# Turning a Mamba scan round: states on the partitions, channels and tokens along the free axis

## The chip, the cores and the metric

The kernel runs on one core of a Trainium2 chip. The metric is the device time of one execution in microseconds, from the first to the last instruction; lower is better. The core's engines are called PE (TensorE; its weight loads are listed as PEld), DVE (VectorE), ACT (ScalarE), POOL (GpSimd) and SP (SyncE, which issues the transfers here).

## What is computed

The kernel runs eight blocks one after the other on a residual of 2048 tokens by 128 features: a gated delta rule, a window attention, a Plücker attention, a ternary feed-forward, a flash attention, a mixture of experts, a bidirectional Mamba and an int8 feed-forward. Only the Mamba block is touched. Cut to what matters, it is, for both directions (m = 1 forward, m = 2 with the tokens flipped):

```
xp, z = split(x @ W_in.T);  xc = silu(causal_conv(xp) + conv_b)      # 256 channels
dt_lo, Bm, Cm = split(xc @ W_xp.T)                                   # 8, 64 states, 64 states
dt = softplus(dt_lo @ W_dt.T + dt_b);  A = -exp(A_log)               # A: 256 x 64
h  = exp(dt[:, :, None] * A) * h + (dt * xc)[:, :, None] * Bm[:, None, :]   # at each token
y  = einsum('ben,bn->be', h, Cm)                                     # sum over the 64 states
out = ((y + xc * Dp) * silu(z)) @ W_out.T
```

There are 8 sequences of 256 tokens. So h has 8 x 256 tokens x 256 channels x 64 states elements in each direction, and each of them goes once through a recurrence along the tokens.

## The kernel before

`bi_mamba` normalises the input, then calls `mamba_inputs`, `mamba_scan` and `mamba_output` for m = 1 and for m = 2. Each call is a block of its own: the next one starts when all engines have ended it. Within a block each engine has its own instruction list, and semaphores (`q[...]`) order the engines among one another.

`mamba_inputs` projects, convolves and makes dt and dtx = dt * xc, four column chunks of 512 tokens (`SCH`) one after the other, with channels on partitions (two halves of 128, `SE`). B and C are projected with their 64 states repeated, and split into three bf16 parts (`high`, `split`: lines 3148 to 3157, 3211 to 3217 and 3240 to 3250), so that TensorE can later copy one state's row to all partitions.

`mamba_scan` has channels on partitions. A step is one state n of one chunk c: 4 x 64 = 256 steps in each direction. In a step
- PE spreads the state's row of B over all partitions (`b_row`, two bf16 matmuls, L3351 and L3352), the row of C likewise (`c_row`), and adds the product hc into banks 0 and 1 (`add_up`, L3368, two f32 matmuls with the identity as weights; a matmul in f32 is listed as two weight loads and two MATMUL records);
- ACT takes the decay exp(A dt) from SBUF to PSUM (`decay`, L3412, two activations of 510 columns; the first token of each sequence keeps a decay of zero) and copies the rows of B (L3418) and part of that of C (L3423) to SBUF;
- POOL multiplies dtx by the row of B (`times_b`, L3454, 128x1024), and a quarter of h by the row of C (L3463);
- DVE runs the recurrence over 1024 elements in one instruction (`scan`, L3488) and multiplies three quarters of h by the row of C (L3496, 128x768).

`mamba_output` gates, reverses the tokens for m = 2, projects (L3529) and adds up; for m = 1 DVE also applies the norm's weights to `k.H` in it.

No transfer runs in these stages but the loads of the weights at their start.

## Time and profile before

| | |
|---|---|
| median of 3 runs | 4789.24 us (4781.74 to 4801.21) |
| the profiled execution: span from first to last instruction | 4788.7 us |
| busy share of the span | PE 82%, PEld 49%, DVE 77%, ACT 53%, POOL 60% |
| Mamba scans in the span | first recurrences near 2988 and at 3881.0 us, 256 in each |
| DMA over the span | 6 GB/s read and written |

In the profile an engine's busy time is the union of its instructions. A group of instructions is a line of the kernel with its engine, operation, output<-inputs, shape and count, then the busy time in us and the mean duration of one in ns, then the idle time of the engine just before them and who ended it. Durations of matmuls include the time until their result is out, so that consecutive ones overlap; what a stream of them costs is read from the distance of their starts.

### The profile page before, as it was taken

To read this page: it belongs to the slowest core of one execution; us is meant where nothing else is said; L and a number is where in the kernel's file an instruction comes from. 1 tells how busy PE (TensorE), PEld (TensorE's weight loads), DVE (VectorE), ACT (ScalarE), POOL (GpSimd) and SP (SyncE) were. 2 spreads that over 40 slices of the span, in tenths; PEclk is the share of its full clock that TensorE was granted. 3 is DMA by queue.
4 is the path that set the end of the run, shared out by engine and by line. 5 is a ranking of instruction groups with operands and counts; after the bars stand their busy time and mean duration, and the time that the engine had idled before them with its cause. 6 is when DMAs were issued, how large, how long until landed. Compare 5 with 4: busy or idle time off the path is not lost. (4 is left out here: it accounts for less than half of the span.)

```text
span 4788.7 us, 76282 instructions
## 1 busy us (share of the span) xinstructions
PE 3918.7 (82%) x20245; PEld 2362.7 (49%) x20365; DVE 3699.5 (77%) x6335; ACT 2539.4 (53%) x5327; POOL 2862.0 (60%) x2784
## 2 busy tenths in 40 slices
PE   5888888888668768677989975888888878888885
PEld 3666666666546556466447742333333423333333
DVE  5777777777468567556148866999999889999995
ACT  3555555555334344423246656666666566666662
POOL 2555555555444144243013343999999669999992
PEclk8999999999878877788999987999999989999997
DMA  1000000000000000000000000000000000000000
GB/s 51 9 9 9 9 9 9 9 9 9 19 0 0 19 0 0 10 0 25 1 18 1 1 14 18 0 0 0 0 0 0 0 0 0 0 0 0 0 0 14
DMA packets 89949, 32.96 MB, mean 7 GB/s; under 512 B 78400, under 2 KB 85968, under 8 KB 88784
## 3 DMA queue, kind: packets, MB, share of 16 engines
q1 hardware_dynamic: 89680, 29.68, 2.6%
q8 instruction: 131, 2.15, 0.2%
q14 instruction: 138, 1.13, 0.1%
HBM read 24.40 MB, written 5.24 MB: 6 GB/s over the span
## 5 line engine op out<-in xcount | busy, mean ns | idle before, releaser
L3454 POOL TENSOR_TENSOR dBx<-dtx,b_row 128x1024 f32<-128x1024 f32 x512 | 1207.3, 2358 | 1.9 <-ACT b_row L3418 1.9
L3488 DVE TENSOR_TENSOR_SCAN h<-banks,dBx 128x1024 f32<-128x1024 f32 x512 | 1169.8, 2285 | 11.8 <-POOL dBx L3454 11.7
L3368 PE MATMUL banks<-hc,ident 128*128 128x512 f32 x2048 | 964.8, 594 | 0.0
L3412 ACT ACTIVATE banks<-dt,alog 128x510 f32<-128x510 f32 x1024 | 661.6, 682 | 1.3 <-DVE h L3488 1.3
L3418 ACT ACTIVATE b_row<-banks 128x512 f32<-128x512 f32 x512 | 305.7, 597 | 567.3 <-PE banks L3352 567.3
L3368 PEld LDWEIGHTS banks<-hc,ident 128*128 128x128 f32 x2048 | 388.4, 190 | 272.7 <-issue 247.4
L3496 DVE TENSOR_TENSOR hc<-h,banks 128x768 f32<-128x768 f32 x512 | 479.4, 936 | 7.3 <-ACT c_row L3423 5.2
L3352 PE MATMUL banks<-bc_lo,selectors 128*128 128x512 bf16 x1024 | 391.1, 382 | 50.9 <-POOLq L3445 41.9
L3463 POOL TENSOR_TENSOR hc<-h,c_row 128x256 f32<-128x256 f32 x512 | 373.2, 729 | 52.0 <-ACT c_row L3423 22.6
L3351 PE MATMUL banks<-bc_hm_c,selectors 128*128 128x512 bf16 x506 | 195.1, 386 | 176.3 <-DVE hc L3496 176.3
L3351 PEld LDWEIGHTS banks<-bc_hm_c,selectors 128*128 (+1 forms) x512 | 49.3, 96 | 424.8 <-issue 424.7
L973 POOL TENSOR_TENSOR weighted<-probs,f 128x1024 f32<-128x1024 f32 x64 | 120.7, 1902 | 215.4 <-DVE f L1024 214.3
L2611 POOL TENSOR_TENSOR out_factors<-out_norms,exponents 128x4 f32<-128x4 f32 x64 | 64.4, 1007 | 284.6 <-DVE out_norms L2776 284.6
L3352 PEld LDWEIGHTS banks<-bc_lo,selectors 128*128 (+1 forms) x1024 | 99.6, 97 | 184.3 <-issue 167.4
L2667 DVE SCALAR_TENSOR_TENSOR qk<-banks,taps,qk 128x255 f32<-128x255 f32 (+2 forms) x384 | 167.2, 477 | 27.6 <-ACT qk L2405 16.4
L2667 DVE SCALAR_TENSOR_TENSOR v_featmajor<-banks,taps,v_featmajor 128x255 f32<-128x255 f32 (+2 forms) x384 | 167.3, 477 | 23.3 <-ACT v_featmajor L2405 12.8
L1766 POOL TENSOR_TENSOR squares<-qkv_ahead 128x1024 f32<-128x1024 f32 x32 | 60.9, 1904 | 189.6 <-ACT qkv_ahead L1702 189.6
L159 POOL MEMSET minus_half<- 128x4 f32 x7 | 0.7, 102 | 269.6 <-POOLq L365 162.9
L2587 POOL TENSOR_TENSOR blocks_inv<-blocks_inv,block_products 64x14 f32<-64x14 f32 (+6 forms) x448 | 117.2, 262 | 63.7 <-issue 0.3
L3351 PE MATMUL banks<-bc_hm_b,selectors 128*128 128x512 bf16 x398 | 152.6, 383 | 3.1 <-ACT b_row L3418 3.1
L2585 POOL TENSOR_TENSOR block_products<-blocks_inv,blocks 64x14 f32<-64x14 f32 (+6 forms) x448 | 113.9, 254 | 67.1 <-issue 5.5
L1211 POOL TENSOR_TENSOR norms<-norms,minus_half 128x64 f32<-128x64 f32 x8 | 84.7, 10593 | 105.9 <-DVE norms L1242 105.9
(458 smaller groups left out, 9084.8 us busy)
## 6 DMA issues: line engine op xcount, KB each, us to landing
delta_blocks<-A_turned SPq DMA_DIRECT2D x256, 8.0 KB, 1.5
inv_turned<-delta_blocks SPq DMA_DIRECT2D x256, 8.0 KB, 1.7
blocks<-delta_blocks SPq DMA_DIRECT2D x32, 64.0 KB, 2.1
delta_blocks<-blocks_inv SPq DMA_DIRECT2D x32, 64.0 KB, 1.9
wh<-in_l1f_wh SPq DMA_DIRECT2D x1, 2048.0 KB, 8.2
wqkv<-in_l0f_wqkv SPq DMA_DIRECT2D x2, 768.0 KB, 4.3
residual<-in_x SPq DMA_DIRECT2D x1, 1024.0 KB, 4.7
wv<-in_l0a_wv SPq DMA_DIRECT2D x1, 1024.0 KB, 7.3
```

Source lines behind the costliest of these rows:

```text
L973: nc.gpsimd.tensor_tensor(blocks(SW[:, u]), blocks(S[:, j % 2, u]), over(f[:, j % 2, 16 * u:16 * u + 16], T // NJ), ALU.mult).then_inc(wei ...
L2587: i = tt(U[:, 0:j, j + 1:], U[:, 0:j, j + 1:], tmp[:, 0:j, 0:n], ALU.add)
L2667: i = stt(out=dst[:, back:], in0=k.bank[4 + n % 2][:, m * T:(m + 1) * T - back], scalar=taps[:, first + m, j:j + 1], in1=dst[:, back:], op ...
L3351: nc.tensor.matmul(k.bank[bank], onto_all(sel[:, 0, bass.ds(n, 1)]), mem[part][:, cols], start=True, stop=False)
L3352: nc.tensor.matmul(k.bank[bank], onto_all(sel[:, which, bass.ds(n, 1)]), mem["lo"][:, cols], start=False, stop=True).then_inc(q[ready], 1)
L3368: i = nc.tensor.matmul(k.bank[e], k.ident[:], hc[:, s, e, :], start=False, stop=False)
L3412: i = nc.scalar.activation(a3[:, :, 1:], d3[:, :, 1:], ACT.Exp, scale=mem["A"][:, e, bass.ds(n, 1)])
L3418: nc.scalar.activation(bsb[:, s, :], k.bank[BBANK], ACT.Copy).then_inc(q["bsb_ready"], 1)
L3454: nc.gpsimd.tensor_tensor(dBx[:, s % NS], dtx[:, :, bass.ds(c * SCH, SCH)], across(bsb[:, s % NS, :], SE), ALU.mult).then_inc(q["dbx_ready ...
L3463: nc.gpsimd.tensor_tensor(hc[:, s % 2, :, DC:], h[:, s % NS, :, DC:], across(csb[:, s % 2, :], SE), ALU.mult).then_inc(q["hcp_ready"], 1)
L3488: v.tensor_tensor_scan(flat(h[:, s % NS]), flat(k.banks[:, at:at + SE, :]), flat(dBx[:, s]), 0.0, ALU.mult, ALU.add).then_inc(q["scanned"], 1)
L3496: v.tensor_tensor(hc[:, s % 2, :, 0:DC], h[:, s, :, 0:DC], across(k.bank[CBANK][:, 0:DC], SE), ALU.mult).then_inc(q["hc_ready"], 1)
```

## The change

The layout of the scan is turned. Partitions now hold 2 channel halves x 64 states; along the free axis lie channels and tokens. A step is four channels of each half for one sequence of 256 tokens, again 128x1024, and 32 steps make a sequence (`NS`), so there are again 256 steps (8 sequences) in each direction.
- `mamba_inputs` no longer splits B and C; they are kept by state in f32 (`copy_b`, `copy_c`). It splits dt into three bf16 parts instead (`high`, `rest`, `middle`, `low`, each 128x1024) and stores dtx and the parts to DRAM (8 transfers and 24 transfers). For m = 1 it also stores `k.X`, `k.H` and the reversed input to DRAM, since the scan uses their place; m = 2 loads the reversed input back.
- SP loads dtx for every step, each channel's row of tokens copied to the 64 state partitions of its half: two transfers a step (`load_dtx`), into four buffers that lie in `k.X` and `k.H`. The parts of dt come once for eight steps (`load_rows`).
- PE spreads dt over the states (`cast`, two bf16 matmuls of 510 columns a step, 96 rows deep), and sums over the states in `chunk`: for each token one f32 matmul with that token's row of C (128x16, `spread`) as weights and the token's column of h, 32 channels with a stride of 256 elements, as the moving operand; 32 of them a step, in four column tiles of the array in turn. `chunk` works LAG = 9 steps behind `cast`.
- ACT makes the decay with four activations of 255 columns a step, PSUM to PSUM (`exps`), lays C out (`build`, four a sequence) and moves the sums out (`move`, one for eight steps).
- POOL only does `times_b`; DVE only the recurrence and, once a sequence, the gate.
- `mamba_output` loads `k.H` and `k.X` back for m = 2, and POOL applies the norm's weights to `k.H` there.

The diff, cut to its core: mostly added lines; what the scan had before is in the listing above.

```diff
@@ mamba_memories, mamba_inputs
+    m["B"], m["C"] = p.sb("b_by_state", [P, B * T]), p.sb("c_by_state", [P, B * T])
+    m["dt_rows"] = nc.dram_tensor("mamba_dt_rows", (SROWS, P // 16, B * T), BF16).ap()
+    m["dtx_rows"] = nc.dram_tensor("mamba_dtx_rows", (B, SE, P, T), F32).ap()
+    m["kept_x"] = nc.dram_tensor("mamba_kept_x", (P, NT, D), F32).ap()
+    m["kept_h"] = nc.dram_tensor("mamba_kept_h", (P, NT, D), F32).ap()
+    m["reversed"] = nc.dram_tensor("mamba_reversed", (P, B, T), F32).ap()
...
+        hi, mid, lo = (p.sb(n, [P, 2, SE, SCH], BF16) for n in ("high", "middle", "low"))
...
+            def _(sp):
+                if m == 1:
+                    sp.dma_start(mem["kept_x"], k.X[:]).then_inc(q["kept"], 16)
+                    sp.dma_start(mem["kept_h"], k.H[:]).then_inc(q["kept"], 16)
+                    sp.wait_ge(q["reversed"], 1)
+                    sp.dma_start(mem["reversed"], rev[:]).then_inc(q["kept"], 16)
+                else:
+                    sp.dma_start(rev[:], mem["reversed"]).then_inc(q["rev_loaded"], 16)
+                def store_dtx(c):
+                    sp.wait_ge(q["dtx_ready"], c + 1)
+                    for e in range(SE):
+                        sp.dma_start(mem["dtx_rows"][2 * c:2 * c + 2, e].rearrange("b p t -> p b t"),
+                                     pairs(dtx[:, e, cols(c)])).then_inc(q["dtx_stored"], 16)
+                def store_rows(c):
+                    sp.wait_ge(q["lo_ready"], c + 1)
+                    for e in range(SE):
+                        for n, part in enumerate((hi, mid, lo)):
+                            at = (e * 3 + n) * 16
+                            sp.dma_start(mem["dt_rows"][at:at + 16, :, cols(c)].rearrange("r k t -> (r k) t"),
+                                         part[:, c % 2, e, :]).then_inc(rows_stored[c % 2], 16)
...
+                store_dtx(0)
+                store_dtx(1)
+                store_rows(0)
+                store_rows(1)
+                store_dtx(2)
+                store_dtx(3)
+                store_rows(2)
+                store_rows(3)
...
-                    for n, (lo, w) in enumerate(((0, P), (P, P), (2 * P, P), (3 * P, R))):
+                    for n, (at, w) in enumerate(((0, P), (P, P), (2 * P, R))):
...
+                if m == 2:
+                    pe.wait_ge(q["rev_loaded"], 16)
+                def copy_b(c):
+                    act.wait_ge(q["bc"], 3 * c + 1)
+                    fn(mem["B"][:, cols(c)], k.bank[4], ACT.Copy).then_inc(q["b_read"], 1)
...
+                def high(c):
+                    pool.wait_ge(q["dtx_ready"], c + 1)
+                    if c >= 2:
+                        pool.wait_ge(rows_stored[c % 2], 96)
+                    nc.gpsimd.tensor_copy(hi[:, c % 2], dt[:, :, cols(c)]).then_inc(q["hi_ready"], 1)
+                def middle(c):
+                    nc.gpsimd.tensor_copy(mid[:, c % 2], en[:, :, cols(c)]).then_inc(q["mid_ready"], 1)
...
+                high(0)
+                high(1)
+                middle(0)
+                middle(1)
+                high(2)
+                middle(2)
+                high(3)
+                middle(3)
...
+                    v.tensor_copy(mem["C"][:, cols(c)], k.bank[5]).then_inc(q["c_read"], 1)
+                        i = v.tensor_tensor(dtx[:, e, cols(c)], dt[:, e, cols(c)], xc[:, e, cols(c)], ALU.mult)
+                    i.then_inc(q["dtx_ready"], 1)
+                def rest(c):
+                    dve.wait_ge(q["hi_ready"], c + 1)
+                    v.tensor_tensor(en[:, :, cols(c)], dt[:, :, cols(c)], hi[:, c % 2], ALU.subtract).then_inc(q["rest"], 1)
+                def low(c):
+                    dve.wait_ge(q["mid_ready"], c + 1)
+                    v.tensor_tensor(lo[:, c % 2], en[:, :, cols(c)], mid[:, c % 2], ALU.subtract).then_inc(q["lo_ready"], 1)
...
+                rest(0)
+                rest(1)
+                low(0)
+                low(1)
+                rest(2)
+                rest(3)
+                low(2)
+                low(3)
@@ mamba_scan
+    NI = T // SJ
+    NS = SUNITS * NI
+    TALL = 16
+    LAG = NI + 1
+        h = p.sb("h", [P, 2, SJ, T])
+        spread = p.sb("c_spread", [P, T, TALL])
+        extra = p.sb("dBx", [P, 2, SSTEP])
+        rows = p.sb("dt_rows", [SROWS, 2, 2, T], BF16)
+        ysb = p.sb("y_tokens", [P, NI, P])
...
+        kept = [flat(a[:])[:, n * SSTEP:(n + 1) * SSTEP] for a in (k.X, k.H) for n in range(2)]
+        dBx = [extra[:, 0], extra[:, 1]] + [flat(k.HT[:])[:, n * SSTEP:(n + 1) * SSTEP] for n in range(2)]
+        SCANS, DBX, CHUNKS, MOVES, CASTS = 4, 4, 2 * NI, 2, 32
+        decay = [k.banks[:, 2 + 2 * s:4 + 2 * s, :].rearrange("p e t -> p (e t)") for s in range(2)]
...
+                def load_rows(u):
+                    tb, jb = u // SUNITS, u % SUNITS
+                    sp.wait_ge(q["cast"], 2 * NI * u + 2 * NI)
+                    sp.dma_start(rows[:, u % 2], mem["dt_rows"][:, 2 * jb:2 * jb + 2, tb * T:(tb + 1) * T]).then_inc(rows_in[u % 2], 16)
+                def load_dtx(n):
+                    tb, jb, i = n // NS, n // NI % SUNITS, n % NI
+                    sp.wait_ge(q["dbx"], n + 1)
+                    for g in range(SE):
+                        src = mem["dtx_rows"][tb, g].rearrange("(a r) t -> a r t", r=8)[2 * i:2 * i + 2, 2 * jb:2 * jb + 2, :]
+                        sp.dma_start(kept[n % 4][g * 64:(g + 1) * 64, :].rearrange("p (a x) -> p a x", a=2),
+                                     src.rearrange("a r t -> a (r t)").partition_broadcast(64)).then_inc(dtx_in[n % 4], 16)
+                load_rows(0)
+                load_dtx(0)
+                sp.dma_start(spread[:].rearrange("p t c -> p (t c)"), k.dram["l3a_zero"].partition_broadcast(P)).then_inc(q["spread_zeroed"], 16)
+                for n in range(1, B * NS):
+                    load_dtx(n)
+                    if n % NI == 5 and n // NI + 1 < B * SUNITS:
+                        load_rows(n // NI + 1)
+                    if m == 1 and n == NS:
+                        load_mamba_weights(k, sp, mem, 2)
+                        sp.wait_ge(weights_in, 208)
+                def cast(tb, l):
+                    n, u, i = tb * NS + l, l // NI, l % NI
+                    if i == 0:
+                        pe.wait_ge(rows_in[u % 2], 16 * (tb * (SUNITS // 2) + u // 2 + 1))
+                    for x in range(2):
+                        pe.wait_ge(q["decayed"], 2 * n + x + 1)
+                        out = k.bank[x].rearrange("p (j t) -> p j t", t=T)[:, :, 1:]
+                        a = 2 * i + x
+                        nc.tensor.matmul(out, mem["sel"][:, 2 * a:2 * a + 2, :].rearrange("r g n -> r (g n)"),
+                                         rows[:, u % 2, :, 1:], start=True, stop=True).then_inc(q["cast"], 1)
+                def chunk(tb, l):
+                    u, i = l // NI, l % NI
+                    if i == 0:
+                        pe.wait_ge(q["scanned"], tb * NS + (u + 1) * NI + SCANS)
+                        pe.wait_ge(q["moved"], tb * SUNITS + u + MOVES)
+                    if u == 0 and i % (NI // 2) == 0:
+                        pe.wait_ge(q["built"], 4 * tb + 4 * i // NI + 2)
+                    for s in range(8):
+                        for c in range(4):
+                            t = i * SJ + c * 8 + s
+                            mm = nc.tensor.matmul(k.bank[OBANK][32 * c:32 * c + TALL, i * SJ:(i + 1) * SJ], spread[:, t, :], h[:, u % 2, :, t],
+                                                  start=s == 0, stop=s == 7)
+                    mm.then_inc(q["chunked"], 1)
+                def by_features(tb):
+                    pe.wait_ge(q["y_read"], tb + 1)
+                    for g in range(SE):
+                        nc.tensor.matmul(by_token(g), mem["diag"][:, g, :], in_eights(xc[:, g, tokens(tb)]), start=g == 0, stop=False)
+                    pe.wait_ge(q["moved"], tb * SUNITS + SUNITS + MOVES)
+                    used = k.ident[:].rearrange("p (c s) -> p c s", s=32)[:, :, 0:TALL]
+                    for i in range(NI):
+                        mm = nc.tensor.matmul(k.bank[YBANK][:, i * 64:(i + 1) * 64], ysb[:, i, :], used, start=False, stop=i == NI - 1)
+                    mm.then_inc(q["y_ready"], 1)
+                def body(tb, first):
+                    for l in range(NS):
+                        cast(tb, l)
+                        if l >= LAG:
+                            chunk(tb, l - LAG)
+                        elif not first:
+                            chunk(tb - 1, l - LAG + NS)
+                        if l == NI + 3 and not first:
+                            by_features(tb - 1)
...
+                def exps(tb, l):
+                    n, u, i = tb * NS + l, l // NI, l % NI
+                    act.wait_ge(q["scanned"], n + SCANS - 1)
+                    for x in range(2):
+                        act.wait_ge(q["cast"], 2 * n + x + 1 + CASTS)
+                        for j in range(2):
+                            at = state(i, 2 * x + j) + 2 * u
+                            e = fn(per_step(decay[l % 2])[:, 2 * x + j, 1:], k.bank[x][:, j * T + 1:(j + 1) * T], ACT.Exp,
+                                   scale=mem["A"][:, at:at + 1])
+                        e.then_inc(q["decayed"], 1)
+                def build(tb, half, g):
+                    if half == 0:
...
+                    dst = spread[lanes, half * n:(half + 1) * n, :].rearrange("p (a s) c -> p a (s c)", s=8)[:, :, 8 * g:8 * g + 7 * 17 + 1:17]
+                    fn(dst, in_eights(mem["C"][lanes, tokens(tb, half * n, n)]), ACT.Copy).then_inc(q["built"], 1)
+                def move(tb, u):
+                    act.wait_ge(q["chunked"], tb * NS + (u + 1) * NI + CHUNKS)
...
+                    fn(out, k.bank[OBANK][:, 0:T].rearrange("p (n a r) -> p n a r", n=NI, r=2),
+                       ACT.Copy).then_inc(q["moved"], 1)
+                builds = {5: (0, 0), 6: (0, 1), 10: (1, 0), 11: (1, 1)}
+                def body(tb, first):
+                    for l in range(NS):
+                        exps(tb, l)
+                        if l % NI == 0:
+                            u = l // NI
+                            if u >= 2:
+                                move(tb, u - 2)
+                            elif not first:
+                                move(tb - 1, u + SUNITS - 2)
+                        if l in builds and not first:
+                            build(tb, *builds[l])
+                act.wait_ge(q["spread_zeroed"], 16)
+                for half in range(2):
+                    for g in range(SE):
+                        build(0, half, g)
+                body(0, True)
...
+                def times_b(tb, l):
+                    n = tb * NS + l
+                    pool.wait_ge(dtx_in[l % 4], 32 * (tb * (NS // 4) + l // 4 + 1))
+                    pool.wait_ge(q["scanned"], n + 1)
+                    nc.gpsimd.tensor_tensor(per_step(dBx[l % 4]), per_step(kept[l % 4]), across(mem["B"][:, tokens(tb)], 4),
+                                            ALU.mult).then_inc(q["dbx"], 1)
+                with pool.Fori(0, B) as tb:
+                    for l in range(NS):
+                        times_b(tb, l)
...
+                def scan(tb, l):
+                    n, u, i = tb * NS + l, l // NI, l % NI
+                    if i == 0:
+                        dve.wait_ge(q["chunked"], tb * NS + u * NI + NI)
+                    dve.wait_ge(q["decayed"], 2 * n + 4)
+                    dve.wait_ge(q["dbx"], n + 1 + DBX)
+                    v.tensor_tensor_scan(flat(h[:, u % 2, 4 * i:4 * i + 4, :]), decay[l % 2], dBx[l % 4], 0.0, ALU.mult,
+                                         ALU.add).then_inc(q["scanned"], 1)
+                def gate(tb):
+                    dve.wait_ge(q["y_ready"], tb + 2)
+                    for g in range(SE):
+                        z = in_eights(sz[:, g, tokens(tb)])
+                        i = v.tensor_tensor(z, by_token(g), z, ALU.mult)
+                def body(tb, first):
+                    for l in range(NS):
+                        scan(tb, l)
+                        if l == 2 * NI and not first:
+                            gate(tb - 1)
@@ mamba_output
+            if m == 2:
+                @block.sync
+                def _(sp):
+                    sp.dma_start(k.H[:], mem["kept_h"]).then_inc(h_back, 16)
+                    sp.dma_start(k.X[:], mem["kept_x"]).then_inc(back, 16)
...
+                    pool.wait_ge(h_back, 16)
+                    nc.gpsimd.tensor_tensor(k.H[:], k.H[:], across(mem["affine"][:, 0, :], NT), ALU.mult)
+                    pool.drain()
+                    nc.gpsimd.tensor_tensor(k.H[:], k.H[:], across(mem["affine"][:, 1, :], NT), ALU.add)
-                if m == 1:
-                    v.tensor_tensor(k.H[:], k.H[:], across(mem["affine"][:, 0, :], NT), ALU.mult)
...
-                    v.tensor_tensor(k.H[:], k.H[:], across(mem["affine"][:, 1, :], NT), ALU.add)
```

## Rows read from the trace of the kernel before

**Rows 1.** The page, busy time of each engine (share of the span, instructions).
```profile
PE 3918.7 (82%) x20245; PEld 2362.7 (49%) x20365; DVE 3699.5 (77%) x6335; ACT 2539.4 (53%) x5327; POOL 2862.0 (60%) x2784
```

**Rows 2.** Windows over the two scans: start:end, length, busy by engine (instructions), PE clock, DMA.
```profile
2988.00:3810.00 822.00, 723.02 (x2082) 305.36 (x2140) 802.83 (x536) 509.67 (x1028) 773.06 (x512) 0.99 0.00 0
...
3880.00:4690.00 810.00, 712.51 (x2016) 296.72 (x2075) 792.84 (x522) 506.02 (x1021) 773.69 (x512) 0.99 0.00 0
```

**Rows 3.** Groups of instructions, 3100 to 3700 us: 193 steps of the first scan.
```profile
L3454 POOL TENSOR_TENSOR dBx<-dtx,b_row 128x1024 f32<-128x1024 f32 x193 | 455.3, 2359 | 0.0
L3488 DVE TENSOR_TENSOR_SCAN h<-banks,dBx 128x1024 f32<-128x1024 f32 x193 | 441.0, 2285 | 0.0
...
L3412 ACT ACTIVATE banks<-dt,alog 128x510 f32<-128x510 f32 x386 | 249.4, 682 | 0.0
L3496 DVE TENSOR_TENSOR hc<-h,banks 128x768 f32<-128x768 f32 x192 | 179.8, 936 | 0.7
...
L3463 POOL TENSOR_TENSOR hc<-h,c_row 128x256 f32<-128x256 f32 x192 | 140.0, 729 | 17.7 <-ACT c_row L3423 7.6 <-PE banks L3368 3.7 <-DVE h L3488 0.2
L3418 ACT ACTIVATE b_row<-banks 128x512 f32<-128x512 f32 x192 | 114.7, 597 | 216.3 <-PE banks L3352 216.3
```

**Rows 4.** Timeline of one step: start in us, duration in us, then the instruction.
```profile
3501.23 2.29 DVE L3488 TENSOR_TENSOR_SCAN h<-banks,dBx 128x1024 f32<-128x1024 f32 x1
...
3501.80 1.29 ACT L3412 ACTIVATE banks<-dt,alog 128x510 f32<-128x510 f32 x2
...
3503.61 0.38 PE L3351 MATMUL banks<-bc_hm_b,selectors 128*128 128x512 bf16 x1
...
3503.82 0.38 PE L3352 MATMUL banks<-bc_lo,selectors 128*128 128x512 bf16 x1
...
3504.36 2.28 DVE L3488 TENSOR_TENSOR_SCAN h<-banks,dBx 128x1024 f32<-128x1024 f32 x1
```

**Rows 5.** Timeline, from the last of the inputs of m = 2 to its first recurrence.
```profile
3873.20 1.29 DVE L3273 TENSOR_TENSOR dtx<-dt,xc 128x512 f32<-128x512 f32 x2
...
3874.91 0.07 DVE L3478 MEMSET banks<- 128x8 f32 x1 [0.41 <-PEq L3072]
...
3878.56 4.65 POOL L3454 TENSOR_TENSOR dBx<-dtx,b_row 128x1024 f32<-128x1024 f32 x2 [0.93 <-ACT b_row L3418]
...
3881.00 2.29 DVE L3488 TENSOR_TENSOR_SCAN h<-banks,dBx 128x1024 f32<-128x1024 f32 x1 [6.03 <-POOL dBx L3454]
```

**Rows 6.** Timeline, the last recurrence of m = 2 and its last gate.
```profile
4675.09 2.29 DVE L3488 TENSOR_TENSOR_SCAN h<-banks,dBx 128x1024 f32<-128x1024 f32 x1
...
4684.15 1.29 DVE L3502 TENSOR_TENSOR silu_z<-banks,silu_z 128x512 f32<-128x512 f32 x2 [3.89 <-PE banks L3378]
```

**Rows 7.** Timeline of PE, small matmuls of the gated delta rule.
```profile
230.89 0.89 PE L2228 MATMUL banks<-inv_turned,steps 64*64 64x32 f32 x24
```

**Rows 8.** Timeline of PE, three tile shapes in the flash attention.
```profile
2569.24 1.14 PE L822 MATMUL banks<-qk_featmajor 64*128 64x256 f32 x8
2570.30 1.09 PE L835 MATMUL banks<-ident,weighted 128*128 128x128 f32 x8
...
2572.19 1.14 PE L855 MATMUL banks<-weighted_keymajor,v 128*64 128x128 f32 x16
```

**Rows 9.** Windows with transfers: weights loading, then two with a row copied to 128 partitions.
```profile
22.00:30.00 8.00, 5.60 (x27) 5.47 (x26) 1.12 (x4) 1.81 (x4) 0.00 (x0) 1.00 1.02 421
1310.50:1311.50 1.00, 0.00 (x0) 0.00 (x0) 0.00 (x0) 0.00 (x0) 0.86 (x1) 0.50 0.76 136
1670.30:1671.40 1.10, 0.00 (x0) 0.00 (x0) 0.00 (x0) 0.00 (x0) 1.10 (x1) 1.00 0.78 256
```

**Rows 10.** The page, transfers: count, size, us from issue to landing.
```profile
wh<-in_l1f_wh SPq DMA_DIRECT2D x1, 2048.0 KB, 8.2
```

**Rows 11.** Timeline of SP, the issue of one transfer.
```profile
1306.97 0.42 SPq L1568 DMA_DIRECT2D qk_scales<-in_l0f_qks  x1
```

**Rows 12.** Groups, inputs of m = 2: the cast to bf16 on POOL.
```profile
L3215 POOL CAST middle<-rest 128x512 bf16<-128x512 f32 x4 | 3.2, 806 | 11.3 <-DVEq L3249 11.3
```

352 lines of the change are left out of this document (112 added, 240 removed).

## The prediction

> **What bounds the kernel now.** I first read the busy shares of the page [rows 1]: PE leads with 82%, but a share over eight different blocks says nothing about one of them, so I went on to the windows of the two scans [rows 2]. There DVE is busy 802.8 of 822 us and POOL 773.1, PE 723.0, ACT 509.7. The groups of a steady stretch [rows 3] show why: per step DVE has a recurrence of 2285 ns and a product of 936 ns and no idle time, POOL has 2359 and 729 ns. The timeline [rows 4] gives the step itself: one recurrence starts at 3501.23, the next at 3504.36. Over the second scan the first of 256 recurrences starts at 3881.00 [rows 5] and the last at 4675.09 [rows 6], 794.1 us for 255 intervals: 3.114 us a step. So DVE sets the pace, POOL is 0.03 us behind, and 2 x 794 = 1588 us of the kernel's 4788.7 go by this step.
>
> **The change, part by part: the step.** With p for the new step in us, the two scans change by 2 x 255 x (p - 3.114). p is the largest of five times.
>
> DVE keeps the recurrence, same size, 2.29 us [rows 3]; its product with C is gone. The gate, once in 32 steps, adds two small products, which I put at 0.8 us together or 0.03 a step from the pair of 1.29 us [rows 6]. 2.32.
>
> POOL keeps its 128x1024 product. Its duration is 2.36 [rows 3], and before the first recurrence two in a row take 4.65 [rows 5], so that 2.33 to 2.36 is the price of one with its gap. Its product with C is gone. 2.36.
>
> ACT: two activations of 510 columns take 1.29 and one 0.68 [rows 3, 4], so the second starts 0.61 after the first. A copy of 512 columns takes 597 ns [rows 3]. Taking about 0.83 ns a column out (an estimate from 510 columns in 0.61 us with a fixed part), one of 255 columns starts 0.40 after the one before it and takes 0.47: two pairs are 1.75, with the wait between them 1.8, and `move` and `build` add 0.1 on average. 1.9, of which the stretch between two recurrences hides all: an `exps` may start when the recurrence two steps back has ended, and has the 2.29 us of the next one.
>
> PE: the two casts start 0.21 us apart, as the bf16 matmuls of 512 columns do now [rows 4]: 0.43. `chunk` is 32 f32 matmuls, hence 64 weight loads and 64 MATMUL records. No row has 16 weight columns and 32 moving ones. The nearest is the gated delta rule: 24 records of 64x32 take 0.89 us, less 0.22 for the last one's latency: 29 ns a record, weight loads (64 columns wide there) included [rows 7]. And 16 records with 128 columns in two column tiles take 1.14, less 0.27: 58 ns each, against 116 between records on the full array (8 records, 0.93 us to the next form) [rows 8]. So column tiles do overlap, and 29 ns is rather high: half of it, 15 ns, is the floor if four tiles overlap fully. Above, a weight load that hides behind nothing would add some 18 ns to it: 47. `chunk` is thus 0.9 to 3.0 us; I take the nearest row, 1.86. The array changes its tile shape twice a step; from 64x128 to 128x128 the next form starts 1.06 us after 8 records that need 0.85 [rows 8], so 0.1 to 0.2 each, 0.2 for both. PE: 2.49, with bounds 1.5 and 3.6. The moving operand's stride of 1 KB stands in no row; nothing excludes that it costs.
> The Trainium skill, "TensorE: Matmul & The Clock Gate", section "Wait — 56ns, not 53.3ns?", says that starts of small matmuls never come closer than about 25 ns. By that rule, read as one per record, `chunk` would be 1.6 and PE 2.2 us (an estimate), and the other engines would set the step.
>
> Transfers: a step writes 128 x 4 KB = 0.52 MB (as the change's `load_dtx` has it), where there was none. With distinct rows the queue moves 421 GB/s over 8 us [rows 9]: 1.25 us a step, hidden. With one row copied to 128 partitions, windows show 136 and 256 GB/s [rows 9], the second partly other traffic: 3.9 and 2.0 us. SP issues a transfer in 0.42 us [rows 11], two a step, hidden. Four buffers give a load about three steps, 7 us, to land. So the bounds are 1.25 and 3.9; here the copied rows are 2 KB long and come from two places, which is nearer to the long distinct ones, and I take 2.3, just hidden.
>
> So p is PE's 2.49, with nearly everything else within 0.2 of it; `chunk` starts a group of eight only when the eighth recurrence and the last `move` are done, for which I add 0.01 a step. p = 2.50, and the scans lose 2 x 255 x 0.614 = 313 us.
>
> **What lies around the step.** End of the inputs, each direction: the split of dt of the last two chunks comes behind the last dtx. DVE's `rest` and `low` are 128x1024, 1.3 us each by the 936 ns for 768 [rows 3]; POOL's casts are 1.4 by the 0.81 us for 512 columns [rows 12]. `high(3)` is queued behind `middle(2)` on POOL, which waits for `rest(2)`: rest, middle, high, rest, middle, low are 1.3+1.4+1.4+1.3+1.4+1.3 = 8.1 us, then six transfers at 0.47 with their pauses behind the six of the chunk before: 12.3, and 1.9 to land: +14 us. The gone splits of B and C (12 DVE operations of 0.7) pay for `copy_c` and the first half of the new ones: 0.
> Start of a scan: now 6.1 us from the first memset to the first recurrence [rows 5]. Then ACT waits for 2 MB of zeros; 2 MB of weights land 8.2 us after issue [rows 10], plus 0.9 until that issue, 1.4 for four `build` and 1.8 for the first decays: 13. +7.
> End of a scan: now 10.4 us from the last recurrence to the end of the gate [rows 6]. Then 2.3 for it, 8 chunks that wait for it (8 x 1.86), 0.6 `move`, 2.0 for 16 records with new weights at 0.116 and latency, 0.8 gate: 20.6. +10.
> That is 31 us in each direction, 62. Loading the reversed input back, 1 MB in front of m = 2's first matmul, is about half of the 8.2 us [rows 10]: +5. Restoring `k.H` on POOL (4 us to load, two products of some 4.6) takes as long as the output stage of m = 2 does now: 0; if that cover fails, +5. The stores of `k.X` and `k.H` and the weights of m = 2 run under inputs and scan: 0, or +5 if they delay `store_dtx`.
> Sum: 4788.7 - 313 + 67 = 4543 us. The profiled execution's span agrees with the median of the runs (4789.2) within 1 us, so nothing is added.
>
> **Rivals.**
> *Engines tighter than PE's row says.* If tiles overlap, POOL's 2.36 sets p: 2 x 255 x 0.754 = 385 less, 4471. It is the lower end of my forecast; with 10 us less around it, 4460.
> *Transfers set the step, and it is still faster.* For it: half of the reads in a window with a copied row were slow [rows 9]. Against it: 421 GB/s with distinct rows. At 190 GB/s, between the windows' 136 and 256, p is 2.76: 4789 + 67 - 181 = 4675.
> The Trainium skill, "SBUF — State Buffer", section "Door 1: The DMA port swizzle (why `[64,N]` ≈ `[32,N]`)", speaks against this change: 64 partitions reach only half of the ports, 196 to 218 GB/s, and two transfers to the two halves do not add up. By that rule a step would need 2.40 to 2.67 us (an estimate), and the kernel 4492 to 4630. No row here has such a transfer.
> *Slower: copied rows are read at 136 GB/s throughout* [rows 9]. All queues read the same 2 KB at once, and the place that holds them serves them one after the other. p = 3.85, 4789 + 67 + 375 = 5231. It decides from p = 3.114 - 67/510 = 2.98 on, that is below 176 GB/s; POOL then waits for dtx, DVE for POOL.
> *Slower: `chunk` at 47 ns a record,* weight load and matmul one after the other, or the stride costs as much: PE 3.0 + 0.63 = 3.63, 4789 + 67 + 263 = 5119. It decides from 37 ns a record on. Against it: no row of small matmuls shows such a sum. The same happens if the PE clock falls to half, since a record then takes twice as long; against that stands the clock of 0.99 in both scans [rows 2] with a PE that would stay as busy as now.
>
> **How the numbers follow.** My forecast (engines set p between 2.36 and 2.6) gets 0.47 and would by itself lie in 4460 to 4595; transfers setting it but faster 0.27; slow copied rows 0.12; slow chunk 0.10; a gain eaten up by both to about nothing 0.04. Slower is 0.21, the same (within 0.5%, 24 us, about what a measurement of this kernel can tell from no change) 0.04, faster 0.75. The range has to leave out most of the two slower cases above it and little below: from 4450 to 4770, the upper end being p = 2.95.
>
> **What would show it.** In the profile after: recurrences 2.5 us apart; PE nearly without idle time within the scans and DVE waiting for PE or ACT; `chunk` records some 29 ns apart; POOL's product unchanged at 2.36. If POOL waits for the dtx transfers, the transfers set the step. A first recurrence some 13 us after the block's start, and some 20 us from the last one to the block's end. The prediction is wrong if the DMA share is near 1 in the scan at under 176 GB/s, or PE's small matmuls are more than 37 ns apart.

## The result and the profile after

The changed kernel takes 5021.0 us (median of 4 runs, 4981.37 to 5029.79), the one before 4792.56 (4 runs, 4781.74 to 4801.21): ratio 1.047, 95% interval 1.043 to 1.051. It is slower by 4.7%; 4543 had been forecast, with 4770 as the upper end.

The page after: busy time of each engine, then the transfers by queue.

```profile
PE 3553.1 (71%) x50301; PEld 2406.5 (48%) x50301; DVE 3276.9 (65%) x5840; ACT 2346.7 (47%) x5437; POOL 2511.8 (50%) x2256
...
q1 hardware_dynamic: 262832, 325.11, 29.2%
q8 instruction: 418, 6.85, 0.6%
```

Against [rows 1] every engine has a smaller share of the span, and the kernel is slower: no engine is the bound all the time. The windows over the two scans, as in [rows 2], say the same.

```profile
3028.00:3902.00 874.00, 514.59 (x16522) 302.79 (x16522) 575.84 (x270) 413.21 (x1082) 595.81 (x255) 0.75 0.75 159
4041.00:4902.00 861.00, 511.38 (x16522) 304.97 (x16521) 576.00 (x270) 412.87 (x1081) 595.70 (x255) 0.76 0.74 160
```

DVE is busy 576 of 861 us where it was busy 792.8 of 810, the DMA engines have a share of 0.74, and 160 GB/s flow where nothing did. The first and the last recurrence of the second scan (the rows that answer to [rows 5, 6]):

```profile
4041.63 4.47 DVE L3572 TENSOR_TENSOR_SCAN h<-banks,dBx 128x1024 f32<-128x1024 f32 x2 [18.43 <-ACT banks L3492]
...
4897.88 4.45 DVE L3572 TENSOR_TENSOR_SCAN h<-banks,norm_featmajor 128x1024 f32<-128x1024 f32 x2
```

The second row holds two recurrences, the last of which starts at 4900.06: 858.4 us for 255 intervals, 3.37 us a step; in the first scan it is 3.42. Before it was 3.114. So the two scans cost 143 us more, not 313 less. These recurrences are not evenly spaced: half of the intervals are 2.23 us or shorter, and one in ten is over 5.5.

Groups of instructions from 4300 to 4900 us, 179 steps of the second scan, to be set beside [rows 3]:

```profile
L3492 ACT ACTIVATE banks<-banks,alog 128x255 f32<-128x255 f32 x720 | 276.6, 447 | 296.4 <-PE banks L3436 280.6 <-DVE h L3572 13.9
L3449 PE MATMUL banks<-h,c_spread 128*16 128x32 f32 x11568 | 218.7, 234 | 189.3 <-issue 188.8
...
L3550 POOL TENSOR_TENSOR dBx<-residual,b_by_state 128x1024 f32<-128x1024 f32 x88 | 206.5, 2364 | 111.7 <-DVE h L3572 111.0 <-DMA residual<-mamba_dtx_rows 0.6
L3572 DVE TENSOR_TENSOR_SCAN h<-banks,dBx 128x1024 f32<-128x1024 f32 x90 | 202.0, 2277 | 127.4 <-ACT banks L3492 103.7 <-PE banks L3449 14.7 <-POOL norm_featmajor L3550 8.7
```

Read from below: POOL waits for DVE's recurrence, DVE for ACT's decays (L3492), ACT for PE's cast (L3436), and PE stood idle in `chunk` (L3449) for 188.8 us with the releaser "issue": nothing that the profile shows as an event held it up. The weight loads (PEld) show where that idle time lies:

```profile
3445.20 0.48 PEld L3449 LDWEIGHTS banks<-h,c_spread 128*16 128x16 f32 x28 [0.28 <-issue]
3449.58 0.57 PEld L3449 LDWEIGHTS banks<-h,c_spread 128*16 128x16 f32 x36 [3.91 <-issue]
3450.25 0.13 PEld L3436 LDWEIGHTS banks<-dt_rows,selectors 96*128 96x128 bf16 x2
3451.22 0.93 PEld L3449 LDWEIGHTS banks<-h,c_spread 128*16 128x16 f32 x64 [0.83 <-issue]
3452.25 0.35 PEld L3436 LDWEIGHTS banks<-dt_rows,selectors 96*128 96x128 bf16 x2
3453.21 0.36 PEld L3449 LDWEIGHTS banks<-h,c_spread 128*16 128x16 f32 x22 [0.62 <-issue]
3456.66 0.68 PEld L3449 LDWEIGHTS banks<-h,c_spread 128*16 128x16 f32 x42 [3.09 <-issue]
```

PE breaks off in the middle of a `chunk`, after 28 of its 64 loads, stands for 3.91 us, goes through 36 + 2 + 64 + 2 + 22 = 126 loads and as many MATMULs, and breaks off again, again in the middle of a `chunk`. No semaphore is waited for at such a place. What is special about it is the count: between the two breaks lie 252 records and four instructions of the sequencer itself (two casts, two of them each), together 256. PE's records repeat with every sequence, so the places can be followed: over six sequences of the second scan they have 18 such block ends each, 108 in all, and each of the 86 pauses of PE over 1 us lies at one of them. Queue q8 carries kind "instruction"; over 100 us (4300 to 4400) the queues moved:

```profile
q1 hardware_dynamic: 9089, 15.43, 68.9%
q8 instruction: 17, 0.28, 1.3%
```

0.28 MB in 17 packets is 16.4 KB each, 256 instructions of 64 bytes. The Trainium skill, "Runtime: NRT & Kernel Launch", section "Instruction fetch mechanics", describes such blocks of 256 instructions, fetched by DMA while the one before is executed, and says that the cost is "mostly hidden". The size agrees with this trace. That it is hidden does not: in the second scan PEld's idle time before L3449 put down to "issue" is 406 us of 859, and at the 108 block ends PE paused for 290 us in 192 steps, 1.5 us a step. From 4200 us on q8 fetched 123 blocks in the second scan. A fetch took 0.98 us (median), and where PE was at rest it went on 1.42 us after the fetch had ended. What is late is the start of the fetch: 3.1 us (median; one in ten over 5.3) after PE had taken up the block before. One of the 18 block ends is the jump back of the loop over the sequences; PE paused there longest, 7.4 us on average.

### The profile page after: what moved, and what is told of

Same layout as the page of the kernel before. It is cut to its first block and busy times, and to the rows that moved or that the text cites. A ratio compares the mean times of both kernels' runs of the same rounds, so it can differ in the third digit from the quotient of the medians.

```text
span 5024.5 us, 130170 instructions
## 1 busy us (share of the span) xinstructions
PE 3553.1 (71%) x50301; PEld 2406.5 (48%) x50301; DVE 3276.9 (65%) x5840; ACT 2346.7 (47%) x5437; POOL 2511.8 (50%) x2256
## 5 line engine op out<-in xcount | busy, mean ns | idle before, releaser
L3492 ACT ACTIVATE banks<-banks,alog 128x255 f32<-128x255 f32 x2048 | 787.8, 447 | 864.2 <-PE banks L3436 796.8
L3449 PE MATMUL banks<-h,c_spread 128*16 128x32 f32 x32768 | 614.6, 234 | 550.0 <-issue 543.7
L3449 PEld LDWEIGHTS banks<-h,c_spread 128*16 128x16 f32 x32768 | 493.1, 115 | 856.1 <-issue 829.9
L3572 DVE TENSOR_TENSOR_SCAN h<-banks,dBx 128x1024 f32<-128x1024 f32 x256 | 576.0, 2279 | 392.5 <-ACT banks L3492 328.7
L3550 POOL TENSOR_TENSOR dBx<-residual,b_by_state 128x1024 f32<-128x1024 f32 x256 | 601.3, 2362 | 356.4 <-DVE h L3572 293.0
L3572 DVE TENSOR_TENSOR_SCAN h<-banks,norm_featmajor 128x1024 f32<-128x1024 f32 x256 | 576.4, 2277 | 226.2 <-ACT banks L3492 213.8
L3550 POOL TENSOR_TENSOR norm_featmajor<-norm,b_by_state 128x1024 f32<-128x1024 f32 x256 | 601.7, 2361 | 215.5 <-DVE h L3572 161.3
L3436 PE MATMUL banks<-dt_rows,selectors 96*128 96x510 bf16 x1024 | 446.7, 506 | 280.7 <-issue 126.3
L3436 PEld LDWEIGHTS banks<-dt_rows,selectors 96*128 96x128 bf16 x1024 | 87.3, 103 | 392.9 <-issue 212.8
L1595 PE MATMUL banks<-wqkv,x_batch 128*128 128x512 f32 x192 | 120.7, 779 | 26.9 <-DVEq L1792 23.8
```

The source lines that it names most:

```text
L1595: i = nc.tensor.matmul(k.bank[4 + n][:], xb[:, t * P:(t + 1) * P], wqkv[:, n * 512:(n + 1) * 512], start=True, stop=True)
L3436: nc.tensor.matmul(out, mem["sel"][:, 2 * a:2 * a + 2, :].rearrange("r g n -> r (g n)"), rows[:, u % 2, :, 1:], start=True, stop=True).the ...
L3449: mm = nc.tensor.matmul(k.bank[OBANK][32 * c:32 * c + TALL, i * SJ:(i + 1) * SJ], spread[:, t, :], h[:, u % 2, :, t], start=s == 0, stop=s ...
L3492: e = fn(per_step(decay[l % 2])[:, 2 * x + j, 1:], k.bank[x][:, j * T + 1:(j + 1) * T], ACT.Exp, scale=mem["A"][:, at:at + 1])
L3550: nc.gpsimd.tensor_tensor(per_step(dBx[l % 4]), per_step(kept[l % 4]), across(mem["B"][:, tokens(tb)], 4), ALU.mult).then_inc(q["dbx"], 1)
L3572: v.tensor_tensor_scan(flat(h[:, u % 2, 4 * i:4 * i + 4, :]), decay[l % 2], dBx[l % 4], 0.0, ALU.mult, ALU.add).then_inc(q["scanned"], 1)
```

## The experiments

Two suspects came out of this: the transfers of dtx are slower than forecast, and PE's instructions come late, perhaps because of the same transfers. Steps below are for the first and second scan, from first and last recurrence; "PEld on issue" is PEld's idle time before the loads of `chunk` in the second scan that is put down to "issue". It has a floor of about 100 us that is no lateness: the three kernels with an eighth of `chunk` and only five blocks on q8 in that scan (e2, e10, e12) show 97 to 111 us. So its differences say more than its size. DMA share is that of q1. Line numbers shift by one or a few between these kernels. The times of e6, e9 and the changed kernel are medians of 4 runs, the others single runs; the kernel before took 4779 to 4798 beside them.

| run | us | step, us | DMA share, GB/s in the 2nd scan | PEld on issue, us |
|---|---|---|---|---|
| changed kernel | 5021.0 | 3.42, 3.37 | 0.73, 161 | 406 |
| e1_no_loads | 4478.6 | 2.36, 2.34 | 0.02, 9 | 74 |
| e2_eighth_chunk | 4742.9 | 2.90, 2.90 | 0.90, 183 | 111 |
| e4_runs_4k | 4669.2 | 2.75, 2.69 | 0.76, 200 | 242 |
| e5_bf16_sum | 4753.6 | 3.00, 2.94 | 0.89, 183 | 142 |
| e6_bf16_sum_runs | 4492.8 | 2.45, 2.42 | 0.87, 223 | 108 |
| e7_all_partitions | 4817.6 | 3.08, 3.06 | 0.88, 174 | 105 |
| e8_bf16_dtx | 4526.6 | 2.42, 2.44 | 0.37, 115 | 146 |
| e9_bf16_both | 4453.9 | 2.35, 2.32 | 0.38, 120 | 102 |
| e10_own_rows | 4450.6 | 2.34, 2.31 | 0.98, 230 | 97 |
| e11_own_rows_full | 4646.5 | 2.64, 2.67 | 0.79, 202 | 240 |
| e12_own_rows_all | 4420.5 | 2.31, 2.30 | 0.74, 230 | 97 |

**No transfers (e1_no_loads).**

```diff
                 for n in range(1, B * NS):
-                    load_dtx(n)
+                    if n < 4:
+                        load_dtx(n)
...
-                    pool.wait_ge(dtx_in[l % 4], 32 * (tb * (NS // 4) + l // 4 + 1))
+                    pool.wait_ge(dtx_in[l % 4], 32)
```

> This kernel leaves work out: dtx is loaded for the first four steps of each scan only, and the later steps multiply with what then lies in the four buffers. Theory F (PE stands still because its next block of instructions arrives late, and it arrives late because it is queued behind the dtx transfers): the stalls of PE inside chunk go, the step falls from 3.39 us to POOL's 2.36 to 2.40, and the time from 5021 to about 5021 - 510 x 1.0 = 4510, between 4490 and 4540. Rival T (the transfers themselves are too slow, 0.52 MB a step at 158 GB/s = 3.3 us, and PE's stalls are harmless): the same 4510, so this run does not tell T from F. Rival S (the block of instructions would be late without any transfer, since 128 records go by in 1.1 us): the step stays at 3.3 to 3.4 us and the time near 5000.

4478.6 us, 2.34 us a step. Some 33,040 PE records as before, the same 143 blocks of instructions, and the stalls are nearly gone: at the 108 block ends PE paused for 45 us instead of 290, and 25 of the 45 lie at the jump back of the loop (4.2 us each). A fetch took 1.11 us here, no less than before, but it began 0.95 us after PE had taken up the block before, instead of 3.1. Rival S falls: without transfers the blocks come in time. The waits of the second scan, first of this run, then of the changed kernel (engine, line and releaser, us in total, times, longest):

```profile
PEld banks L3450 <- issue: 73.5, 240, 1.5
...
ACT banks L3493 <- PE banks L3437: 54.9, 38, 4.5
```

```profile
PEld banks L3449 <- issue: 406.3, 340, 9.6
ACT banks L3492 <- PE banks L3436: 394.1, 158, 12.3
```

The timeline of this run also gives PE's own price of a step undisturbed:

```profile
4103.05 1.09 PE L3450 MATMUL banks<-h,c_spread 128*16 128x32 f32 x64
...
4104.18 0.39 PE L3437 MATMUL banks<-dt_rows,selectors 96*128 96x510 bf16 x1
```

64 MATMUL records and the change to the next form take 1.13 us, so `chunk` is far below the 1.86 us of the forecast. 2.35 us is POOL's product, and with it the rival "engines tighter" is priced: it had been put at 4471.

**Few instructions, all transfers (e2_eighth_chunk).** `chunk` sums for 4 of its 32 tokens.

```diff
-                    for s in range(8):
+                    for s in range(1):
...
-                                                  start=s == 0, stop=s == 7)
+                                                  start=True, stop=True)
```

> This kernel leaves work out: chunk sums over the states for 4 of its 32 tokens, so PE has 20 records a step instead of 132; all transfers stay. Theory F: PE asks for a block of 256 records once in 13 steps, the stalls go, and the step falls to what the transfers or POOL allow, 2.4 to 2.6 us: 4510 to 4620. Rival T (transfers bind at 158 GB/s): the step stays at 3.3 to 3.4 us, 4980 to 5020.

4742.9 us, 2.90 us a step, between the two expectations. Five blocks of instructions are fetched in the second scan instead of 143, and POOL now waits for the transfers:

```profile
POOL norm_featmajor L3550 <- DMA norm<-mamba_dtx_rows: 86.9, 85, 2.8
```

```profile
q1 hardware_dynamic: 79043, 135.22, 89.6%
```

With the 54.2 us of the other two buffers POOL waits 141 us for transfers, which is the whole of 255 x (2.895 - 2.344). So both suspects are real. Transfers alone set 2.90 us (T had the mechanism, and a price 0.4 too high), and the changed kernel's step is 0.47 to 0.52 us longer still. That does not make two waits one behind the other in the changed kernel: there POOL waits for transfers only 34 us of the second scan (27.4 and 6.6), and PE's pauses at the block ends, 1.3 us a step more than in e1, cover by themselves the 1.02 us by which the step is longer. The slow transfers act there mostly by making the blocks late.

**Half the instructions, all the work (e5_bf16_sum).**

```diff
-        h = p.sb("h", [P, 2, SJ, T])
-        spread = p.sb("c_spread", [P, T, TALL])
+        h = p.sb("h", [P, 2, SJ, T], BF16)
+        spread = p.sb("c_spread", [P, T, TALL], BF16)
...
-                sp.dma_start(spread[:].rearrange("p t c -> p (t c)"), k.dram["l3a_zero"].partition_broadcast(P)).then_inc(q["spread_zeroed"], 16)
...
-                act.wait_ge(q["spread_zeroed"], 16)
...
                 v.memset(k.bank[OBANK], 0.0)
+                v.memset(spread[:], 0.0)
```

> h and the row of C are in bf16, so that each of chunk's 32 matmuls is one weight load and one MATMUL record instead of two and two: 68 records a step instead of 132; the transfers stay (DVE fills the zeros of the weights). Theory F: a block of 256 records lasts 3.8 steps instead of 1.9; with some 6.6 us from one block to the next when PE is held up, that is 1.75 us a step, and POOL or the transfers set 2.4 to 2.7 us: 4510 to 4670. Rival T: step unchanged at 3.3 to 3.4 us, 4980 to 5020.

4753.6 us, 2.94 to 3.00 a step: nearly the time of the kernel with an eighth of the sum. Halving the instructions (81 blocks instead of 143; the time of `chunk` falls too, from 1.09 to 0.62 us) is enough to take nearly the whole of that cost away, and what stays is the transfers' 2.9. The expectation of 4510 to 4670 missed it because it took 2.4 to 2.7 as the transfers' own limit.

**Longer runs (e4_runs_4k).**

```diff
-                        src = mem["dtx_rows"][tb, g].rearrange("(a r) t -> a r t", r=8)[2 * i:2 * i + 2, 2 * jb:2 * jb + 2, :]
-                        sp.dma_start(kept[n % 4][g * 64:(g + 1) * 64, :].rearrange("p (a x) -> p a x", a=2),
-                                     src.rearrange("a r t -> a (r t)").partition_broadcast(64))
+                        src = mem["dtx_rows"][tb, g, 4 * (n % NS):4 * (n % NS) + 4, :]
+                        sp.dma_start(kept[n % 4][g * 64:(g + 1) * 64, :], src.rearrange("r t -> (r t)").partition_broadcast(64))
```

> The dtx of a step is read as one run of 4 KB for each partition instead of two of 2 KB (the four rows are other channels' than the step's, so the values differ, the bytes do not). Theory F, with the delay made by the bytes that are queued ahead of the block of instructions: little changes, the step stays at 3.2 to 3.5 us, 4950 to 5060. Theory F, with the delay made by the number of queued pieces (half as many now): the step falls to 2.7 to 3.0, 4670 to 4820. Rival T with a cost per run of 2 KB: likewise 2.7 to 3.0.

4669.2 us, 2.69 to 2.75 a step: the case "cost per piece". The same bytes in half as many pieces go at 200 GB/s with a share of 0.76, PEld's time on issue falls from 406 to 242 us, and PE's pauses at the block ends from 290 to 169. This run alone does not say whether the transfers or the blocks gave the gain; the next one does.

**Both taken away (e6_bf16_sum_runs).** The bf16 sum, and dtx stored in the order of the steps:

```diff
-    m["dtx_rows"] = nc.dram_tensor("mamba_dtx_rows", (B, SE, P, T), F32).ap()
+    m["dtx_rows"] = nc.dram_tensor("mamba_dtx_rows", (B, SE, 4, 16, 2, T), F32).ap()
...
-                        sp.dma_start(mem["dtx_rows"][2 * c:2 * c + 2, e].rearrange("b p t -> p b t"),
-                                     pairs(dtx[:, e, cols(c)])).then_inc(q["dtx_stored"], 16)
+                        for b in range(2):
+                            for r in range(2):
+                                sp.dma_start(mem["dtx_rows"][2 * c + b, e, :, :, r].rearrange("j q t -> q j t"),
+                                             pairs(dtx[r::2, e, cols(c)])[:, b]).then_inc(q["dtx_stored"], 16)
...
-                        src = mem["dtx_rows"][tb, g].rearrange("(a r) t -> a r t", r=8)[2 * i:2 * i + 2, 2 * jb:2 * jb + 2, :]
-                        sp.dma_start(kept[n % 4][g * 64:(g + 1) * 64, :].rearrange("p (a x) -> p a x", a=2),
-                                     src.rearrange("a r t -> a (r t)").partition_broadcast(64))
+                        src = mem["dtx_rows"][tb, g, jb, 2 * i:2 * i + 2]
+                        sp.dma_start(kept[n % 4][g * 64:(g + 1) * 64, :], src.rearrange("a r t -> (a r t)").partition_broadcast(64))
```

> The bf16 sum of the run before, and dtx stored in DRAM in the order in which the steps read it, so that a partition's four rows are one run of 4 KB with the right values (32 stores a direction instead of 8). The runs so far left two costs: transfers of 2 KB runs set 2.9 us when PE's instructions are few, and late instructions set 2.7 us when the runs are 4 KB. If both are real and separate (theory F), taking away both leaves POOL's 2.36 to 2.45 us: 4490 to 4560. If it was one cost with two names, nothing is gained over the better of the two: 2.65 to 2.75 us and 4660 to 4700.

4492.8 us (4 runs, 4489.53 to 4508.5), 0.938 of the kernel before (0.934 to 0.941), 2.42 to 2.45 a step. Either measure alone leaves 2.7 or 2.9, both together nearly POOL's own time: two costs, not one with two names.

**Half the bytes (e8_bf16_dtx, e9_bf16_both).** dtx goes through DRAM in bf16, stored in the order of the steps and loaded into four small buffers of its own; e9 has the bf16 sum as well.

```diff
-                        i = v.tensor_tensor(dtx[:, e, cols(c)], dt[:, e, cols(c)], xc[:, e, cols(c)], ALU.mult)
+                        i = v.tensor_tensor(dtx16[:, e], dt[:, e, cols(c)], xc[:, e, cols(c)], ALU.mult)
...
-        kept = [flat(a[:])[:, n * SSTEP:(n + 1) * SSTEP] for a in (k.X, k.H) for n in range(2)]
+        kept = [p.sb(f"dtx_spread{n}", [P, SSTEP], BF16)[:] for n in range(4)]
```

> dtx goes through DRAM in bf16, in the order of the steps, so a step's transfers are 0.26 MB in runs of 2 KB; the sum stays in f32 with its 132 records a step. Theory F (the block of instructions is late by what is queued ahead of it): with half the bytes ahead the wait halves; the step is 2.36 to 2.5 us, 4490 to 4580. If late instructions do not depend on the bytes ahead but on transfers being there at all: 2.7 us, as in the run with 4 KB runs, 4670.

4526.6 us with the whole f32 sum and its 143 blocks: 2.42 to 2.44 a step, PEld on issue for 146 us, pauses at the block ends 103 us. With a DMA share of 0.37 the blocks come more nearly in time.

> dtx in bf16 through DRAM and the sum in bf16. Neither late instructions nor transfers should be left; POOL's product and DVE's recurrence set the step at 2.35 us: 4475 to 4520. A POOL product that takes a bf16 operand could be slower or faster than 2.36 us; by theory F it moves the step with it.

4453.9 us (4441.6 to 4470.52), 0.928 of the kernel before (0.924 to 0.932): the fastest of those that compute everything, with dtx, h and C rounded to bf16, which the kernel before does not do. Its step of 2.32 to 2.35 is that of the kernel without transfers. It came out 21 us below the lower expectation's end; POOL's product with a bf16 operand takes 2149 ns instead of 2364, and DVE's recurrence is then the longest.

```profile
L3552 POOL TENSOR_TENSOR norm_featmajor<-dtx_spread,b_by_state 128x1024 f32<-128x1024 bf16 x128 | 274.1, 2149 | 5.4 <-DVE h L3575 1.1
```

**Why the transfers are slow (e7, e10, e12).** All with an eighth of `chunk`, so that transfers are the limit. e7 fills all 128 partitions from the first half's rows in one transfer:

```diff
-                    for g in range(SE):
-                        src = mem["dtx_rows"][tb, g].rearrange("(a r) t -> a r t", r=8)[2 * i:2 * i + 2, 2 * jb:2 * jb + 2, :]
-                        sp.dma_start(kept[n % 4][g * 64:(g + 1) * 64, :].rearrange("p (a x) -> p a x", a=2),
-                                     src.rearrange("a r t -> a (r t)").partition_broadcast(64)).then_inc(dtx_in[n % 4], 16)
+                    src = mem["dtx_rows"][tb, 0].rearrange("(a r) t -> a r t", r=8)[2 * i:2 * i + 2, 2 * jb:2 * jb + 2, :]
+                    sp.dma_start(kept[n % 4].rearrange("p (a x) -> p a x", a=2),
+                                 src.rearrange("a r t -> a (r t)").partition_broadcast(P)).then_inc(dtx_in[n % 4], 16)
...
```

> Beside the kernel with an eighth of chunk (4743 us, 2.90 us a step, so with the transfers alone as its limit): one transfer a step writes all 128 partitions, from the first half's rows (the other half's values differ), instead of two that write 64 partitions each; the runs stay at 2 KB and the bytes at 0.52 MB. If the limit is that 64 partitions can take only about half of what 128 can, as the Trainium skill says (SBUF: State Buffer, section Door 1): above 250 GB/s, the step 2.36 to 2.45, 4480 to 4530. If the limit is the many copies of one row that are read: 2.9 us or more, 4740 or more.

4817.6 us, 3.06 to 3.08 a step at 174 GB/s: slower than with 64 partitions a transfer (4742.9, 183 GB/s). The first theory, that 64 partitions are the limit here, fails, though e7 also has each row read by twice as many partitions. e10 leaves the 64 partitions and gives each rows of its own:

```diff
-                        src = mem["dtx_rows"][tb, g].rearrange("(a r) t -> a r t", r=8)[2 * i:2 * i + 2, 2 * jb:2 * jb + 2, :]
-                        sp.dma_start(kept[n % 4][g * 64:(g + 1) * 64, :].rearrange("p (a x) -> p a x", a=2),
-                                     src.rearrange("a r t -> a (r t)").partition_broadcast(64))
+                        src = mem["dtx_rows"][tb].rearrange("g (p r) t -> g p (r t)", r=2).rearrange("g p x -> p g x")
+                        sp.dma_start(kept[n % 4][g * 64:(g + 1) * 64, :].rearrange("p (a x) -> p a x", a=2), src)
```

> With an eighth of chunk (4743 us with the copied rows, 2.90 us a step at 183 GB/s): the same two transfers a step, 64 partitions each, the same 2 KB runs and bytes, but each partition reads rows of its own instead of all 64 reading the same ones (the values differ). If the copies of one row are what is slow: the transfers are hidden, the step is 2.36 to 2.45 us, 4480 to 4530. If 64 partitions or 2 KB runs are what is slow: unchanged, 2.9 us, 4740.

4450.6 us, 2.31 to 2.34 a step: same pieces, same bytes, same partitions, and the transfers are hidden. Reading the same row 64 times is what cost 2.90 us; here a row is read twice in a step, once for each half. The edit changes one thing more, which no run separates: the 32 steps of a sequence now read the same 256 KB. But the DMA engines are at their limit here too, which the transfers of the second scan show, first of e10, then of e12, in which one transfer writes all 128 partitions with rows of their own:

```profile
q1 hardware_dynamic: 78740, 134.68, 97.9%
```

```diff
...
+                    at = tb if tb < B - 1 else tb - 1
+                    src = mem["dtx_rows"][at:at + 2].rearrange("b g p t -> (b g p t)").rearrange("(a p x) -> p a x", a=2, p=P)
+                    sp.dma_start(kept[n % 4].rearrange("p (a x) -> p a x", a=2), src).then_inc(dtx_in[n % 4], 16)
...
```

> With an eighth of chunk, rows of their own for all 128 partitions (the values differ) and one transfer of 0.52 MB a step in 2 KB runs, instead of two that write 64 partitions each. With those two the DMA engines were busy 0.98 of the time at 229 GB/s, a piece of 2 KB took 0.137 us on average, and the step was 2.31 to 2.34 us. If that rate is the limit of writing 64 partitions (the Trainium skill, SBUF: State Buffer, section Door 1): pieces take 0.08 to 0.10 us, the DMA share falls to 0.6 to 0.75 and the step stays at POOL's 2.3 to 2.4 (4430 to 4500). If the number of partitions does not matter: share 0.95 or more, pieces 0.13 us or more, the same step and time.

```profile
q1 hardware_dynamic: 74709, 134.64, 74.3%
```

The same bytes in the same time with 74% of the engines' time instead of 98%; a piece of 2 KB takes 0.106 us on average instead of 0.137. So two transfers of 64 partitions were dearer than one of 128. The Trainium skill ("SBUF — State Buffer", section "Door 1: The DMA port swizzle (why `[64,N]` ≈ `[32,N]`)") has this for 64 partitions, and the two runs agree; at a share of 0.98 e10 gives 230 GB/s, a little above its 196 to 218. The width alone is not isolated: e10's two transfers read the same rows, while e12 reads each row once. With copied rows that limit is not reached, and the copies set 183.

**Late instructions, other transfers (e11_own_rows_full).** e10's edit on the changed kernel with its whole sum.

> The changed kernel with the whole sum (132 records a step) and rows of its own for each partition (the values differ), so the same number of pieces and bytes stands in the queues. If late instructions come from the time that queued transfers take: with faster transfers the wait shrinks as with 4 KB runs or more, the step is 2.4 to 2.7 us, 4500 to 4660. If they come from the number of pieces or bytes, however fast they go: 3.0 us or more, 4800 or more.

4646.5 us, 2.64 to 2.67 a step, PEld on issue for 240 us instead of 406. The number of pieces, the bytes and the instructions are those of the changed kernel; only the transfers are faster. So the lateness goes with the time that the queued transfers take to land. The four kernels with loads and the whole f32 sum line up by it, e1 without loads stands below them:

| run | landing of a dtx transfer, us | start of a fetch after PE took up the block before, us | pauses at the 108 block ends, us |
|---|---|---|---|
| changed kernel | 6 | 3.1 | 290 |
| e11_own_rows_full | 4.4 | 2.1 | 177 |
| e4_runs_4k | 4.4 | 2.0 | 169 |
| e8_bf16_dtx | 3.0 | 1.9 | 103 |
| e1_no_loads | | 0.95 | 45 |

With few instructions the same transfers allow 2.31 (e10), so with the whole sum the step is still some 0.35 us longer here.

## Why the prediction was wrong

**The step that failed** is the list of times of which p is the largest. It has a time for DVE, POOL, ACT, PE and the transfers, and none for fetching PE's instructions: that term was put at nothing without a reason. `chunk` is counted there as 64 weight loads and 64 MATMUL records and priced by their distance alone; that they are also 8 KB of program a step, which comes through the same DMA engines that the change fills with dtx, was not seen. The page of before showed 131 packets of kind "instruction" on q8 in the whole kernel; the new one has 418. What the runs showed in its place: PE rests at the ends of its blocks for 1.5 us a step, against 0.2 without loads. The step is 0.47 to 0.52 us longer than with the same transfers and few instructions, about 250 us in all (510 x 0.49), and this alone turns a small gain into the loss: with the transfers as slow as they are and few instructions the kernel takes 4743 us, inside the range.

**The transfers, 2.3 us,** were mis-sized: 2.90 measured, 181 to 183 GB/s. The forecast chose a value near the long distinct rows between the bounds 1.25 and 3.9. e10 shows that the other property decided: the same transfers with distinct rows are hidden. The rival "transfers set the step" (190 GB/s, 2.76 us, 4675) had this nearly right by itself, and "copied rows at 136 GB/s" had the cause with too high a price. The direct reading of the rows, one row copied to many partitions at 136 and 256 GB/s [rows 9], was better evidence than the run length for which it was left. The run length counts as well: with 4 KB runs and half the instructions the step is 2.42 to 2.45 (e6).

**PE's `chunk`, 1.86 us,** was mis-sized the other way: 1.03 to 1.13. Its records start 13.7 ns apart on average, not 29, about the lower bound of 15 that the text gives for four tiles that overlap fully; the stride of 1 KB brought no visible price, though no run had another stride. The floor of about 25 ns between starts that the prediction cites from the Trainium skill does not hold for these matmuls in four column tiles. "Slow chunk" falls, and with it the reason given for "PE clock at half", that a record then takes twice as long: the two windows below, one at either level of the clock, hold a `chunk` of 64 records each, and the timeline has 1.10 and 1.09 us for them. The clock does change the casts. From the start of the two casts to the next `chunk` it is 0.96 us at a clock of 0.50 (3459.44 to 3460.40) and 0.54 at 1.00 (3461.76 to 3462.30). Even so PE needs 2.0 us a step at the lower level, less than POOL's 2.36, and in e2 the clock is 0.50 throughout with a shorter step. So the mean clock of 0.76 in the scans (0.99 before) is not what sets the step; what it adds where PE catches up after a pause was not separated.

```profile
3451.20:3452.30 1.10, 1.10 (x66) 0.98 (x65) 0.00 (x0) 1.10 (x4) 0.88 (x1) 0.50 1.11 136
...
3462.30:3463.40 1.10, 1.10 (x66) 1.00 (x65) 1.10 (x1) 1.10 (x4) 1.10 (x1) 1.00 0.57 177
```

```profile
3451.22 1.10 PE L3449 MATMUL banks<-h,c_spread 128*16 128x32 f32 x64
...
3459.44 1.03 PE L3436 MATMUL banks<-dt_rows,selectors 96*128 96x510 bf16 x2
...
3460.40 1.43 PE L3449 MATMUL banks<-h,c_spread 128*16 128x32 f32 x64
...
3461.76 0.60 PE L3436 MATMUL banks<-dt_rows,selectors 96*128 96x510 bf16 x2
...
3462.30 1.09 PE L3449 MATMUL banks<-h,c_spread 128*16 128x32 f32 x64
```

**Right were** DVE (2.28 for 2.29), POOL (2.36), and ACT, where four activations take 1.54 us for an estimated 1.75. All three are seen at work in e1: step 2.35, time 4479 against the 4471 of the rival "engines tighter".

**What lies around the step** was 67 us and came to 78: to the first recurrence 26 more than before (21 forecast), between the scans 41 (36), after the last 10.9 (10). The parts of m = 2: from the last product of dtx to the next block 13 us (14 forecast); from there to the first recurrence 19.1 instead of 6.1, 6 more than forecast, since the zeros are issued 3.7 us after the block's start instead of 0.9, ACT can use them 10.7 us later where 8.2 was taken, and ACT's table load of 1.28 us is exposed; the last recurrence to the end of the gate 18.5 instead of 10.4. The rows of that start:

```profile
4026.22 0.59 SPq L3417 DMA_DIRECT2D c_spread<-in_l3a_zero  x1
...
4036.96 1.73 ACT L3504 ACTIVATE c_spread<-c_by_state 64x128 f32<-64x128 f32 x4 [42.37 <-DMA c_spread<-in_l3a_zero]
4038.70 1.28 ACT L3492 ACT_TABLE_LOAD   x1
```

With 143 and 78 us the profiled execution would be at 5010; the other 14 us lie before the Mamba block, which begins 14.3 us later in that execution than before. In e1 to e12 it begins between 11 us earlier and 22 us later than before, so single runs that differ by 20 us are not told apart by their times; the steps tell them apart.

**The sum again, with what was measured:** 4788.7 + 78 + 510 x (2.35 - 3.113) = 4478 for engines alone (e1: 4479), + 510 x 0.55 = 4758 with the transfers of copied rows (e2: 4743; what lies around its scans is some 20 us shorter, as an eighth of `chunk` ends sooner), + 510 x 0.49 = 5008 with the late instructions, + 14 = 5022. The split holds in this order only, few instructions first: with the whole sum, other rows for the transfers alone take 0.7 to 0.8 us off the step (e11).

**What stays open.** That the fetch of a block starts late because of the transfers is shown (e1, e4, e8, e11 against the changed kernel). Where it waits is not: behind them in the DMA engines' queues, or for the memory that they read; the trace has no record of when a block is asked for. Why copies of one row are slow was narrowed to what is read (e10 against e2), no further. The changed kernel's 0.73 share at 161 GB/s, against 0.90 at 183 in e2, fits two costs that feed one another: while PE stands, no buffer comes free, and the queue has less to do.

## What to carry to other kernels

An engine's program is a transfer too. Count the instructions that a step adds, 64 bytes each, and where a stage streams both data and many small instructions, look at the packets of kind "instruction" and at idle time put down to "issue" at places without waits that lie 256 instructions apart; halving the records (bf16 instead of f32 here) or the bytes took most of it away. Idle time put down to "issue" has a floor that is no stall; measure it in a run with few instructions. A row copied to many partitions is not priced by the rate of distinct rows: measure it as such, in the runs in which it will be read. When nearly every term of a sum is within 0.2 us of the largest, as here, a term that is missing can decide the time.

## What the runs showed of the hardware

Four column tiles of 16 columns took small f32 matmuls every 13.7 ns, each with its weight load, at either level of the granted clock (0.50 and 1.00). One row read by 64 partitions in 2 KB runs: 183 GB/s (e2); by 128 partitions, 174 (e7); in 4 KB runs, at least 223 (e6). Rows of their own: 230 GB/s at a DMA share of 0.98 in two transfers of 64 partitions (e10), and at 0.74 in one of 128 (e12), where the step and not the transfers sets the rate. A block of 256 PE instructions lasts 1.8 to 1.9 steps here; its fetch takes about 1 us once it has begun, begins 0.95 us after PE has taken up the block before without loads and 3.1 with them, and PE goes on 1.4 us after its end. At a jump back of the loop PE rested 4.2 us without loads (e1) and 7.4 with them.
